# Layer 2's recurrence: weights from ramps on ScalarE, products on VectorE, the second half interleaved

## The reference, cut to what matters

```
k, v = time_shift(h, mix_k) @ Wk_t.T, time_shift(h, mix_v) @ Wv_t.T
r = sigmoid(time_shift(h, mix_r) @ Wr_t.T)
# for each sequence and channel, over the 256 steps; aa = 0, pp = -inf at first
p   = max(pp, u + k_t);  e1, e2 = exp(pp - p), exp(u + k_t - p)
out = (e1 * aa + e2 * v_t) / (e1 + e2 + 1e-8)
p2  = max(pp, k_t);      e1b, e2b = exp(pp - p2), exp(k_t - p2)
aa  = e1b * aa + e2b * v_t
pp  = p2 + log(e1b + e2b + 1e-8)
# after it
x = x + r * out
h2 = layer_norm(x)
x = x + sigmoid(time_shift(h2, cmix_r) @ Wr_c.T) * (square(relu(time_shift(h2, cmix_k) @ Wk_c.T)) @ Wv_c.T)
```

## Time and profile before

| | us |
|---|---|
| median of 3 runs | 2234.5 (2232.88 to 2235.41) |
| the profiled execution's own time | 2244.19 |
| its span in the profile | 2242.4 |
| PE busy / DVE busy / ACT busy / POOL busy | 1885.0 / 1558.1 / 1285.2 / 652.3 |
| mean granted TensorE clock (1 is 2.4 GHz) | 0.911 |

### The profile page before, as it was taken

One profiled execution on the slowest core, in us unless ns is written; L12 is line 12 of the kernel. 1 busy time (PEld: TensorE's weight loads), 2 busy tenths in 40 slices (PEclk: granted clock), 3 DMA queues, 4 the chain that ended last, 5 costly groups with the idle time before them and its releaser, 6 DMA issues.

```text
span 2242.4 us, 37692 instructions
## 1 busy us (share of the span) xinstructions
PE 1885.0 (84%) x13296; PEld 1250.2 (56%) x13296; DVE 1558.1 (69%) x3633; ACT 1285.2 (57%) x2737; POOL 652.3 (29%) x616
## 2 busy tenths in 40 slices
PE   7999775988999999949974288999997997589886
PEld 5777562446777777524452165566665676434465
DVE  5777685866777677458758947989997456478543
ACT  5777533776888878617755236677665212247622
POOL 3223003203544434342004532444343001221043
PEclk9999896998999999969987599999999898779898
DMA  4000004411000000035101000000000100354102
GB/s 196 1 1 2 1 1 129 138 37 38 1 1 1 1 1 1 1 90 155 58 1 77 0 1 1 1 2 1 1 1 22 36 1 1 120 164 114 57 24 78
DMA packets 80153, 87.37 MB, mean 39 GB/s; under 512 B 6578, under 2 KB 70115, under 8 KB 79073
## 3 DMA queue, kind: packets, MB, share of 16 engines
q1 hardware_dynamic: 78625, 82.49, 11.7%
q0 software_dynamic: 1344, 2.49, 0.4%
HBM read 54.39 MB, written 30.70 MB: 38 GB/s over the span
## 4 chain that ended last, share of the span: by engine, by line
PE 53%; DVE 29%; ACT 7%; issue 6%; POOL 2%; DMA 2%; SPq 0%; another core or an unknown queue 0%; DVEq 0%; ACTq 0%; POOLq 0%
PE bank L469 45%; DVE scratch L1221 5%; PE bank L653 2%; ACT XN L1996 2%; PE bank L2934 2%; PE bank L368 2%; DVE scratch L3052 1%; DVE scratch L3072 1%; PE bank L693 1%; DVE stats L245 1%; DVE XN L3092 1%; DVE scratch L1608 1%; DVE w_keep L1895 1%; ACT L2074 1%; DVE w_early L2501 1%
## 5 line engine op out<-in xcount | busy, mean ns | idle before, releaser
L469 PE MATMUL bank<-scratch 64*128 64x256 bf16 (+7 forms) x3056 | 340.2, 306 | 67.5 <-DMA scratch<-parts 39.4
L1221 DVE TENSOR_REDUCE scratch<-bank 128x2 f32<-128x512 f32 x384 | 244.6, 686 | 82.4 <-PE bank L469 79.8
L469 PEld LDWEIGHTS bank<-scratch 64*128 64x128 bf16 (+4 forms) x3056 | 184.1, 122 | 195.7 <-DVE scratch L1221 73.9
L469 PE MATMUL bank<-w_keep,scratch 128*128 128x128 f32 (+4 forms) x1760 | 245.4, 330 | 18.4 <-DVE scratch L1938 4.1
L1307 ACT ACTIVATE w_keep<-bank 128x512 f32<-128x512 f32 x384 | 212.6, 597 | 52.0 <-PE bank L469 44.3
L469 PE MATMUL bank<-XNT,w_keep 128*128 128x256 f32 (+4 forms) x800 | 238.0, 437 | 4.5 <-POOL w_keep L2135 2.2
L469 PEld LDWEIGHTS bank<-w_keep,scratch 128*128 128x128 f32 (+3 forms) x1760 | 182.7, 184 | 84.0 <-issue 55.6
L469 PEld LDWEIGHTS bank<-XNT,w_keep 128*128 128x128 f32 x800 | 149.9, 197 | 57.7 <-issue 28.4
L469 PE MATMUL bank<-w_early,scratch 64*128 64x256 f32 (+3 forms) x1152 | 164.8, 346 | 20.4 <-ACT w_early L3152 8.7
L469 PEld LDWEIGHTS bank<-w_early,scratch 64*128 64x128 f32 (+3 forms) x1152 | 120.0, 185 | 66.4 <-issue 25.6
L469 PE MATMUL bank<-w_keep 128*32 128x256 f32 (+1 forms) x1600 | 124.3, 386 | 11.3 <-ACT w_keep L1307 5.4
(11 more groups left out here) (452 smaller groups left out, 3898.7 us busy)
## 6 DMA issues: line engine op xcount, KB each, us to landing
scratch<-parts SPq DMA_DIRECT2D x24, 1024.0 KB, 5.0
parts<-scratch SPq DMA_DIRECT2D x192, 96.0 KB, 2.3
parts<-scratch SPq DMA_DIRECT2D x96, 64.0 KB, 2.1
w_early<-pack_l3f SPq DMA_DIRECT2D x1, 5206.0 KB, 14.9
w_keep<-pack_l2f SPq DMA_DIRECT2D x1, 2124.0 KB, 12.6
w_early<-pack_mamba SPq DMA_DIRECT2D x1, 2120.0 KB, 19.3
w_keep<-pack_l2x SPq DMA_DIRECT2D x1, 2049.0 KB, 7.9
w_keep<-taps SPq DMA_DIRECT2D x4, 512.0 KB, 5.3
```

Source lines behind the costliest of these rows:

```text
L469: return pe.matmul(out, lhsT, rhs, start=start, stop=stop, skip_group_check=True)
L1221: dve.tensor_reduce(neg[:, :, h], self.k.bank[5 - g % 2][:, :].rearrange("p (t s) -> p t s", s=S), AXX, ALU.max, negate=True).then_inc(*s. ...
```

## The change

On VectorE (`ahead_dve`), x = k less the *previous* running maximum is formed once. ScalarE makes both weights from it: two ramps, relu(x) and relu(-x), and then exp(-ramp) of each (`ramps_act`); d = exp(-relu(x)) and c = exp(-relu(-x)) are the two weights, since max(a, b) - a = relu(b - a). The logarithm of the previous sum is subtracted from x (`level_dve`), and the second weights come from that; the third weights are the same ramps with bias `r_u` and `minus_u`. GpSimd's differences and products are gone: the products are on VectorE. The reciprocal is gone: ScalarE takes Ln of the denominator and Exp of its negative (`inverse_act`), and the two layer norms inside take Ln and Exp(-0.5 ...) (`log_root_act`) in place of Sqrt and reciprocal. Two preloads of a table set that has both Ln and Exp stand in ScalarE's list. The work of `LAST` is moved between that of `FIRST` on VectorE, and partly behind norm "second"; PE turns part 3 ahead of up 1 and norm "later" ahead of down 1. In the diff a line of "..." marks lines left out; the old functions stand above.

```diff
@@
+    minus_u = tmp2(k, 1)
@@
     def fold_pool(pool):
+        pool.tensor_scalar(minus_u, w["r_u"], -1.0, None, ALU.mult)
         for name, (mix, now, prev, less) in folded.items():
@@
-    def first_decay_dve(dve, part):
-        (_, _, _, d, _, _, _), (pm, _, _) = streams[part]
+    def ahead_dve(dve, part):
+        (kk, v, r, d, c, x, num), (pm, sp, aa) = streams[part]
+        k3 = b3(kk)
+        dve.wait_ge(*s.stacked.at("in", part, 0))
+        scan(dve, part, pm, k3, k3, BEFORE_ALL, ALU.max, ALU.max).then_inc(*s.vector.up("p", part))
         dve.wait_ge(*s.vector.at("p", part))
-        dve.tensor_tensor(b3(d), pm[:, :, 0:S], pm[:, :, 1:PADDED], ALU.subtract).then_inc(*s.formed.up("d", part))
+        dve.tensor_tensor(b3(x), k3, pm[:, :, 0:S], ALU.subtract).then_inc(*s.formed.up("x", part))
 
     def sums_dve(dve, part):
-        (kk, v, r, d, c, m, num), (pm, sp, aa) = streams[part]
+        (kk, v, r, d, c, x, num), (pm, sp, aa) = streams[part]
         dve.wait_ge(*s.weighed.at("first", part))
         scan(dve, part, sp, b3(d), b3(c), 0.0, ALU.mult, ALU.add).then_inc(*s.vector.up("s", part))
-
...
+        dve.wait_ge(*s.vector.at("s", part))
+        dve.tensor_tensor(b3(num), b3(d), sp[:, :, 0:S], ALU.mult).then_inc(*s.vector.up("ds", part))
+    def raised_dve(dve, part):
+        (kk, v, r, d, c, x, num), (pm, sp, aa) = streams[part]
+        dve.wait_ge(*s.vector.at("ds", part))
+        dve.tensor_tensor(num, num, c, ALU.max).then_inc(*s.vector.up("larger", part))
+        dve.wait_ge(*s.vector.at("larger", part))
+        dve.scalar_tensor_tensor(out=c, in0=num, scalar=1e-8, in1=c, op0=ALU.mult, op1=ALU.add).then_inc(*s.vector.up("raised", part))
+        dve.wait_ge(*s.vector.at("raised", part))
+        scan(dve, part, sp, b3(d), b3(c), 0.0, ALU.mult, ALU.add).then_inc(*s.vector.up("s2", part))
+    def level_dve(dve, part):
+        (kk, v, r, d, c, x, num), _ = streams[part]
+        dve.wait_ge(*s.scalar.at("log", part))
+        dve.tensor_tensor(x, x, num, ALU.subtract).then_inc(*s.formed.up("x2", part))
+    def weigh_dve(dve, part):
+        (kk, v, r, d, c, x, num), (pm, sp, aa) = streams[part]
+        dve.wait_ge(*s.weighed.at("second", part))
+        dve.wait_ge(*s.stacked.at("in", part, 1))
+        dve.tensor_tensor(c, c, v, ALU.mult).then_inc(*s.vector.up("cv", part))
+        dve.wait_ge(*s.vector.at("cv", part))
+        scan(dve, part, aa, b3(d), b3(c), 0.0, ALU.mult, ALU.add).then_inc(*s.vector.up("a", part))
+    def whole_dve(dve, part):
+        (kk, v, r, d, c, x, num), _ = streams[part]
+        dve.wait_ge(*s.weighed.at("third", part))
+        dve.scalar_tensor_tensor(out=x, in0=num, scalar=1e-8, in1=kk, op0=ALU.add, op1=ALU.add).then_inc(*s.vector.up("den", part))
+    def gate_dve(dve, part):
+        (kk, v, r, d, c, x, num), (pm, sp, aa) = streams[part]
+        dve.wait_ge(*s.vector.at("a", part))
+        dve.wait_ge(*s.vector.at("den", part))
+        dve.tensor_tensor(b3(num), b3(num), aa[:, :, 0:S], ALU.mult).then_inc(*s.vector.up("da", part))
+        dve.tensor_tensor(v, v, kk, ALU.mult).then_inc(*s.vector.up("vc", part))
+        dve.wait_ge(*s.vector.at("vc", part))
+        dve.wait_ge(*s.vector.at("da", part))
+        dve.tensor_tensor(num, num, v, ALU.add).then_inc(*s.vector.up("num", part))
+        dve.wait_ge(*s.scalar.at("inverse", part))
+        dve.wait_ge(*s.vector.at("num", part))
+        dve.tensor_tensor(num, num, x, ALU.mult).then_inc(*s.vector.up("out", part))
+        dve.wait_ge(*s.vector.at("out", part))
+        dve.wait_ge(*s.stacked.at("in", part, 2))
+        dve.tensor_tensor(num, num, r, ALU.mult).then_inc(*s.divided.up("gated", part))
 
     def residual_dve(dve, tag, parts):
 
@@
         if tag == "later":
             dve.wait_ge(*s.scaled.at("second", NT // 2 - 1))
         variance_dve(k, dve, tag)
-        inverse_dve(k, dve, tag)
+        dve.wait_ge(*s.deviation.at(tag))
         shift_dve(k, dve, tag)
 
     INPUTS = (("r_wk", 0, ACT.Copy), ("r_wv", 1, ACT.Copy), ("r_wr", 2, ACT.Sigmoid))
@@
         up_pe(e, 0)
         down_pe(e, 0)
         num_pe(e, 2)
+        num_pe(e, 3)
         up_pe(e, 1)
-        num_pe(e, 3)
+        turn_half_pe(e, "later", (2, 3))
         down_pe(e, 1)
-        turn_half_pe(e, "later", (2, 3))
         e.wait_ge(*s.formed.at("later", 3))
         for q in (2, 3):
             up_pe(e, q)
@@
         affine_dve(e, "first", "r_g1", "r_b1", PARTS)
         scale_dve(k, e, "outer", k.X, k.XN, range(NT))
         for part in PARTS:
-            (kk, v, r, d, c, m, num), (pm, sp, aa) = streams[part]
...
+            ahead_dve(e, part)
+        for part in FIRST:
             sums_dve(e, part)
-        raised_dve(e, FIRST)
...
+            raised_dve(e, part)
+        level_dve(e, 0)
+        sums_dve(e, 2)
+        level_dve(e, 1)
+        raised_dve(e, 2)
+        weigh_dve(e, 0)
+        sums_dve(e, 3)
+        whole_dve(e, 0)
+        weigh_dve(e, 1)
+        whole_dve(e, 1)
+        raised_dve(e, 3)
+        gate_dve(e, 0)
+        gate_dve(e, 1)
+        for part in LAST:
+            level_dve(e, part)
         residual_dve(e, "second", FIRST)
         scale_dve(k, e, "second", k.XN, O2, range(0, NT // 2))
+        weigh_dve(e, 2)
         affine_dve(e, "second", "r_g2", "r_b2", FIRST)
-        gate_dve(e, LAST)
+        weigh_dve(e, 3)
+        for part in LAST:
+            whole_dve(e, part)
+        for part in LAST:
+            gate_dve(e, part)
         residual_dve(e, "later", LAST)
         scale_dve(k, e, "later", k.XN, O2, range(NT // 2, NT))
         affine_dve(e, "later", "r_g2", "r_b2", LAST)
@@
-    def first_weights_act(act, part):
...
+    def ramps_act(act, tag, part, x, down, up, first_bias, second_bias):
+        act.activation(down, x, ACT.Relu, bias=first_bias).then_inc(*s.lowered.up(tag, "down", part))
+        act.activation(up, x, ACT.Relu, bias=second_bias, scale=-1.0).then_inc(*s.lowered.up(tag, "up", part))
+        act.wait_ge(*s.lowered.at(tag, "down", part))
+        act.activation(down, down, ACT.Exp, scale=-1.0)
+        act.wait_ge(*s.lowered.at(tag, "up", part))
+        act.activation(up, up, ACT.Exp, scale=-1.0).then_inc(*s.weighed.up(tag, part))
+    def weights_act(act, tag, part):
+        (kk, v, r, d, c, x, num), _ = streams[part]
+        act.wait_ge(*s.formed.at("x" if tag == "first" else "x2", part))
+        if tag == "second":
+            act.wait_ge(*s.vector.at("s2", part))
+        if tag == "third":
+            ramps_act(act, tag, part, x, num, kk, w["r_u"], minus_u)
+        else:
+            ramps_act(act, tag, part, x, d, c, 0.0, 0.0)
+    def inverse_act(act, part):
+        (_, _, _, _, _, x, _), _ = streams[part]
+        act.wait_ge(*s.vector.at("den", part))
+        act.activation(x, x, ACT.Ln).then_inc(*s.lowered.up("den", part))
+        act.wait_ge(*s.lowered.at("den", part))
+        act.activation(x, x, ACT.Exp, scale=-1.0).then_inc(*s.scalar.up("inverse", part))
+    def log_act(act, part):
+        (_, _, _, _, _, _, num), (_, sp, _) = streams[part]
+        act.wait_ge(*s.vector.at("s2", part))
+        act.activation(b3(num), sp[:, :, 0:S], ACT.Ln).then_inc(*s.scalar.up("log", part))
+    def log_root_act(act, tag):
+        act.wait_ge(*s.variance.at(tag))
+        act.activation(k.rs[:, :], k.moments[:, 2, :], ACT.Ln, bias=k.small[:, 0:1], scale=1.0 / P).then_inc(*s.lowered.up("root", tag))
+        act.wait_ge(*s.lowered.at("root", tag))
+        act.activation(k.rs[:, :], k.rs[:, :], ACT.Exp, scale=-0.5).then_inc(*s.deviation.up(tag))
 
     def act(e):
         table_act(k, e, ACT.Sqrt)
@@
         again_act(k, e, "first")
         again_scale_act(k, e, "first", O)
         scale_act(k, e, "outer", k.X, k.XN, range(NT))
-        for part in PARTS:
+        e.preload_act_table_set("natural_log_exp_and_others")
+        for part in (0, 1, 2):
             input_act(e, part, 0)
-        for part in PARTS:
...
+        weights_act(e, "first", 0)
+        input_act(e, 3, 0)
+        weights_act(e, "first", 1)
+        input_act(e, 0, 1)
+        weights_act(e, "first", 2)
+        input_act(e, 1, 1)
+        weights_act(e, "first", 3)
+        input_act(e, 2, 1)
+        input_act(e, 3, 1)
+        log_act(e, 0)
+        log_act(e, 1)
+        weights_act(e, "second", 0)
+        weights_act(e, "second", 1)
+        weights_act(e, "third", 0)
+        weights_act(e, "third", 1)
+        log_act(e, 2)
+        inverse_act(e, 0)
+        inverse_act(e, 1)
         for part in PARTS:
             input_act(e, part, 2)
-        logs_act(e, FIRST)
...
+        e.preload_act_table_set("natural_log_exp_and_others")
+        log_act(e, 3)
+        weights_act(e, "second", 2)
+        weights_act(e, "second", 3)
+        log_root_act(e, "second")
+        scale_act(k, e, "second", k.XN, O2, range(0, NT // 2))
+        weights_act(e, "third", 2)
+        weights_act(e, "third", 3)
+        relu_act(e, 0)
+        relu_act(e, 1)
```

(67 more changed lines are left out.)

93 lines of the change are left out of this document (removed).

## The result

The changed kernel took **2193.7 us** (median of 4 runs, 2191.64 to 2196.54) beside 2234.8 for the kernel before (4 runs): ratio 0.9818 [0.9801, 0.9835], 41 us faster.

A forecast was written before the change was run, and what follows sets the result against it. The prediction took VectorE's list up to the affine of norm "second", then PE's list, as the bound. 32.2 us less there plus 0.5 behind gave 32.7 off the median 2234.5: 2202 us, 8-in-10 range 2196 to 2211.

The forecast's parts named there:

- the sum: Whole change: 32.2 us off VectorE's work up to the affine, 0.5 off PE's behind it, 32.7 us less.
- the list: VectorE's work from its first scan to the affine's end of norm "second": 53.3 us, 32.2 less than before.
- 37 x 0.72: VectorE ahead of the affine: 37 operations outside scans and norm at 0.72 us each, 26.6 us together.
- the waits of 1.7: VectorE waiting for ScalarE behind the first scan, since part 3's copy stands behind part 0's weights: 1.7 us.
- the part behind it: PE's work after the affine: 1.0 us of idle time gone, 0.5 added for square 3, net 0.5 less.
- the start: Stretch before VectorE's first scan: one more small GpSimd operation makes the first matmul 0.1 to 0.2 us later.
- a microsecond or two: Elsewhere in the program: the clock granted there moves a run by this much (2232.9 to 2235.4).
- The idle 1.00: PE's idle time ahead of up 2: goes because norm "later" has its affine under down 1, 1.0 us less.
- the wait for square 3: PE ahead of down 0: square 3's relu stands behind part 3's inverse on ScalarE, 0.5 us more.
- Rival A: PE behind down 0: part 3 gated some 5 us late, clock restart costs about 2.3 again; 2209 us, chance 20%.
- Rival B: ScalarE becomes the bound ahead of the norm: sets of 3.5 us lose about 8.4 us; 2210 us, chance 4%.
- rival C: VectorE's long instruction forms are not GpSimd's doing, so its work is simply added; slower, 2263 us, chance 3%.

The follow-up runs named there:

- before without GpSimd: Kernel before with GpSimd's 32 recurrence instructions put on VectorE at the same places, nothing else changed: 2234.66 us beside 2243.41, ratio 0.9961.
- the loaded run: Changed kernel with two useless 128x512 activations added to each weight set on ScalarE: 2202.23 us beside 2232.78, ratio 0.9865.

## Why the prediction was off

**What failed.** The gain was 41.1 us where the sum had 32.7: 8.4 too little. 3.0 of them are in the stage: the list came out 2.7 shorter than its sum, since the steps "37 x 0.72" and the waits of 1.7 were sized too high, the part behind it 1.2 shorter, and the start 0.95 longer, which the sum had at nothing. 5.4 are in the step that took the rest of the program as unchanged, but for "a microsecond or two" of clock. The stage's error alone would have left the time within the range (2199.1, below), so this last step is the one that broke it, and what moved the rest of the program stays open.

**Bound and place: right.** The gain in the stage, 35.7 us, is VectorE's list (-35.0) and what lies behind it (-1.7), less 0.95 at the start. The affine ended at 1247.67 (forecast 1248).

**Where the list's 35 went.** From the kernel before, GpSimd's contention is an estimated 24.8, less 18.3 for its work taken over. Undone singly in the changed one, reciprocals are 7.0 and the order 2.8 (such shares needn't add up exactly). The rest, some 18.7, I can only name as the new form (one difference for two weights, no minimum and maximum): it had no run of its own from the kernel before. Its count fits: the list of "before without GpSimd" has 28 two-tensor operations that the new form does without (4 first differences, 12 for the second weights, 12 for the third), at 0.60 to 0.72 a step 17 to 20 us.

**The list's size: 53.3 forecast, 50.6 measured; 2.7 too much.** Waits for ScalarE behind the first scan were 0.8 instead of 1.7. The 37 operations took 25.1 instead of 26.6: 14 of them step in 0.58 to 0.61, since they don't hold up the next instruction. The earlier trace rows gives one step of the dependent kind (1232.21 to 1232.94), and I used it for all. The scans took 18.7 (forecast 18.8), the norm 5.9 (6.2).

**Behind: -1.7 for -0.5.** The idle 1.00 went as forecast, and the wait for square 3 was 0.35, not 0.5. What the sum had at nothing is the turn of norm "later": it steps on in 0.87 (1272.47 to 1273.34) instead of 1.57, since its scalings now end 1.9 us ahead of it. Down 1 and up 2 are 0.3 shorter together. Rival A did not come: part 3 was gated as down 0 ended. Its reasoning was near, since VectorE waited 2.85 for the inverse of part 2 where 1.6 was laid out.

**Start: +0.95 for +0.15**, unexplained. VectorE's ten scalings beside GpSimd's folds took 4.15 instead of 3.33. It is the change's doing, since every kernel made from the changed one has a start of 14.88 to 14.91 and every one made from the kernel before 13.94; by what means wasn't tested.

**Two of the rivals' sums are off**, without effect on the forecast. Rival B's losses (3.4 and 8.4) use a slack of 5.1 where the text says 7.5; the loaded run shows 12 - 6.3 = 5.7. In rival C, 1248.2 + 50 is 1298, not 1297, and PE's wait of "some 10" enters as 12.

**What put the time below the range** is not in the stage. The prediction took the 9.7 us between the profiled execution and the runs of before as noise without a place. It has one: in the last stage of the program PE stood with "issue" as the only cause ahead of it. PE in the kernel before's profile:

```profile
2177.79 1.16 PE L469 MATMUL bank<-w_keep,w_early 128*128 128x320 f32 x3 [1.15 <-issue]
2179.95 1.46 PE L469 MATMUL bank<-w_keep,w_early 128*128 128x320 f32 x2 [1.00 <-issue]
2182.74 1.22 PE L469 MATMUL bank<-w_keep,w_early 128*128 128x320 f32 x2 [1.32 <-issue]
```

The last 396 matmuls take 72.4 to 74.0 us from first start to last in that profile and in those of eleven experiments, and 61.9 to 62.0 in the changed kernel's first profile and in the four taken on one chip, whatever the kernel. So these 12 us belong to the launch or chip. Both first medians look free of them: 2234.8 stands near the 2232.8 of the kernel before on that one chip, not near the 2243.4 to 2243.9 on the others. That the same 9.7 was taken off on both sides did no harm, by luck: the prediction had no reason for it.

What remains is the 5.4 between 41.1 and 35.7, in the rest of the program: median less the profile's stage is 2076.7 for the first runs of before and 2071.4 for the first of after, but 2072.6 to 2074.9 for five kernels on the chip free of those 12 us, before's among them. The profiles show no place for it. The span less the stage and less those matmuls is 2010.6 before and 2010.3 after, and 2006.1 and 2009.8 in the two repeats of the changed kernel, so launches of one kernel differ there by about as much. By the stage alone the time would be 2234.8 - 35.7 = 2199.1, within the range. Why the rest moved by five is open.
